# The batch loops of projection, attention and output of an adaLN transformer block, written out on every engine

## The chip, the core and the metric

The kernel runs on one core of one Trainium2 chip. The core has five engines, each with its own instruction sequencer and its own instruction stream: TensorE (PE, matrix products; its weight loads are listed as PEld), VectorE (DVE), ScalarE (ACT), GpSimd (POOL) and SyncE (SP, which here only issues DMAs). The streams meet at semaphores. The metric is the device time of one execution in microseconds; less is better.

## What is computed

The reference is a transformer block with adaptive layer norm: 16 batches of 1024 tokens, model width 256, 16 heads of 16, causal attention with rotary embedding, then a sparse feed-forward part over the first 2048 tokens.

```python
x = L0_attn_x                                   # (16, 1024, 256)
mod = (silu(c) @ wmod).reshape(16, 6, 1, -1)    # sa, ca, ga, sb, cb, gb
h = layernorm(x) * (1 + ca) + sa
# attention: q, k, v = layernorm(h) @ W + b; rope on q and k
scores = einsum('bhid,bhjd->bhij', q, k) / sqrt(16)      # causal mask
out = softmax(scores) @ v
x = x + ga * (h + out @ Wo + bo)
h = layernorm(x) * (1 + cb) + sb
x = x + gb * ffn(h)          # 8 experts, 512 gathered tokens each, gelu
```

## The kernel before

`build` runs five stages one after the other, each in a block of its own: `phase0` (weights and modulation), `phase1` (layer norms, projection, rotary embedding, splitting q and k into bf16 parts), `phase2` (attention), `phase3` (output projection and residual) and `phase4` (feed-forward). The text calls the middle three the projection, attention and output stages. The order of every engine's work is written by hand: each engine has a function that issues its own instructions and waits on semaphores whose target values are worked out from the batch number.

In these three stages the batches beyond the first few are driven by a hardware loop, `eng.Fori(lo, hi)`: the body stands once in the engine's program, a register holds the batch number, and at the end of the body the sequencer adds one and branches back. Every wait whose target depends on the batch needs that target computed in a register. Every engine has a loop of its own, and they are not tied to one another by anything but the work's semaphores.

- Projection: `run` (L343) writes out batches 0 to 2 and the last two, and loops over `it` from 1 to 6, two batches in a turn, on DVE, ACT, POOL and PE (L350). SP loops over `it` from 1 to 5 (L400). On DVE each batch is eight tiles of `rotate` (L474, L475, L481), `take_rest` (L490), the layer norm's statistics (`take_h`, L443) and `front_xn` (L461). POOL makes `h` (L625, L627) and the third part of q and k (L641).
- Attention: the work is 64 units, four head groups in each of 16 batches. A unit on PE has 40 score tiles (`scores_for_exp`, L1060), among them the filling of the maxima's banks for the unit two ahead (`fill`, L1035 and L1042), and 10 products of probabilities with v (`weigh`, L1079). ACT takes the exponentials of the 40 tiles (L997), DVE reduces the maxima (L951), POOL cuts the diagonal (L890). `steps` (L817) drives SP, POOL and DVE: batch 0 written out, a loop over batches 1 to 14, batch 15 written out. PE has the same shape (L1107 to L1113), and ACT writes out batch 0 and loops over 1 to 15 (L1009). A turn of these loops is one batch, four units.
- Output: `loop` (L1146) writes out batches 0 and 1 and loops over `it` from 1 to 7, two batches in a turn, on DVE, ACT and PE (L1149). SP loops from 1 to 6 (L1170). DVE's last step of each tile is L1203.

A loop of n turns takes its branch back n - 1 times and falls through at the last. For PE that is 5 times in the projection stage, 13 times in the attention stage and 6 times in the output stage. ACT's attention loop has 15 turns, so it branches back once more than PE's.

Of the kernel before, what the change touches and what calls it, by code (L numbers as in the profile page):

```python
# [27 lines left out]
NG = 4  # L28
# [245 lines left out]
def phase1(nc, x, ps, ident, rope, w_all, bias3, ones3, mods_d, resid_d, q_d, k_d, v_d):  # L274
    B, L, D = x.shape
# [7 lines left out]
    with ExitStack() as ctx:  # L283
# [59 lines left out]
        def run(eng, front, both, tail):  # L343

            front(batch(0, 0))
            both(batch(0, 1), batch(0, 0), first=True)
            both(batch(0, 2), batch(0, 1))
            with eng.Fori(1, B // 2 - 1) as it:  # L350
                both(batch(it, 1), batch(it, 0))
                both(batch(it, 2), batch(it, 1))
            last = B // 2 - 1
            both(batch(last, 1), batch(last, 0), more=False)
            both(None, batch(last, 1), more=False)
            tail(batch(last, 1))

        @block.sync
        def _(sp):
# [37 lines left out]
            load(batch(0, 2))  # L397
            step(0, 0)
            step(0, 1)
            with sp.Fori(1, B // 2 - 2) as it:  # L400
                step(it, 0)
                step(it, 1)
            step(B // 2 - 2, 0)
# [313 lines left out]
def phase2(nc, B, L, ps, ident, mask, q_d, k_d, v_d, max_d, att_d):  # L717
# [49 lines left out]
    AHEAD = 2  # L767

    with ExitStack() as ctx:
# [27 lines left out]
        LAST = B - 1  # L797
# [19 lines left out]
        def steps(eng, prologue, step, epilogue=lambda: None):  # L817

            prologue()
            for n in range(NG):  # L820
                step(unit(0, n), unit(0, n + AHEAD))
            with eng.Fori(1, LAST) as b:
                for n in range(NG):
                    step(unit(b, n), unit(b, n + AHEAD))
            for n in range(NG):
                step(unit(LAST, n), unit(LAST, n + AHEAD) if n + AHEAD < NG else None)
            epilogue()

        @block.sync
# [149 lines left out]
        def _(act):  # L979
# [24 lines left out]
                        copy_out(un, 0)  # L1004
                    exp(un, i)

            for n in range(NG):
                step(unit(0, n), None, first=(n == 0))
            with act.Fori(1, B) as b:  # L1009
                for n in range(NG):  # L1010
                    step(unit(b, n), None)
            copy_out(unit(LAST, NG - 1), 1)

        @block.tensor
        def _(pe):
# [88 lines left out]
                        weigh(prior(un), NPC + i - LAG)  # L1104

            prologue()
            for n in range(NG):  # L1107
                step(unit(0, n), unit(0, n + AHEAD), first=(n == 0))
            with pe.Fori(1, LAST) as b:
                for n in range(NG):  # L1110
                    step(unit(b, n), unit(b, n + AHEAD))
            for n in range(NG):
                step(unit(LAST, n), unit(LAST, n + AHEAD) if n + AHEAD < NG else None)  # L1113
            for i in range(NPC - LAG, NPC):
                weigh(unit(LAST, NG - 1), i)

# [2 lines left out]
def phase3(nc, B, L, D, ps, ident, wo, ones3, mods_d, out_bias_d, resid_d, att_d, sum_d, out):  # L1119
# [5 lines left out]
    with ExitStack() as ctx:  # L1125
# [20 lines left out]
        def loop(eng, work):  # L1146
            for p in range(2):
                work(p, 0, p)
            with eng.Fori(1, B // 2) as it:  # L1149
                for p in range(2):  # L1150
                    work(it * 2 + p, it, p)

# [6 lines left out]
        @block.sync  # L1159
        def _(sp):  # L1160
            def store(b, p, dst):
                sp.wait_ge(x2_done, b * T + T)
                sp.dma_start(dst.rearrange("(t p) d -> p t d", p=P), x2[:, p]).then_inc(stored[p], DMA)

            load(sp, 0, 0)
            load(sp, 1, 1)
            for p in range(2):
                store(p, p, sum_d[p * L:(p + 1) * L] if p < SB else out[p])
                load(sp, p + 2, p)
            with sp.Fori(1, B // 2 - 1) as it:  # L1170
                for p in range(2):
                    store(it * 2 + p, p, out[it * 2 + p])
                    load(sp, it * 2 + p + 2, p)
            for p in range(2):
                store(B - 2 + p, p, out[B - 2 + p])
            for p in range(2):
                sp.wait_ge(stored[p], DMA * (B // 2))
# [444 lines left out]
```

## Time and profile before

| | us |
|---|---|
| median of 3 runs | 3348.53 |
| range of the runs | 3348.07 to 3353.41 |
| the profiled execution | 3348.41 |
| its span, first to last instruction | 3346.70 |

So 1.7 us of the profiled execution lie outside its span, and it stands 0.1 us below the median. Durations and stretches below are from this execution. Projection takes about 79 to 745 us of the span, attention 825 to 2716 us, output 2733 to 3001 us. [...]

### The profile page before, as it was taken

The numbers are of one execution on the slowest core, as the hardware profiler recorded it, in microseconds if no ns is written. First come the engines' busy times: TensorE is split into PE (matmuls) and PEld (weight loads), VectorE is DVE, ScalarE is ACT, GpSimd is POOL, SyncE is SP. The second block draws the span as 40 slices with busy tenths as digits, with TensorE's granted clock in tenths as the row PEclk, the third lists the DMA queues.
The fourth block names the chain that finished last, engine by engine and source line by source line (L and its number), as shares of the span: only waits on it lengthen the run. The fifth ranks groups of instructions, "written<-read, shape, count | busy, mean of one in ns | idle before, by whom it ended". The sixth has DMA issues, their size and how long they took to land. (4 is left out here: it accounts for less than half of the span.)

```text
span 3346.7 us, 60748 instructions
## 1 busy us (share of the span) xinstructions
PE 2990.9 (89%) x18199; PEld 1411.5 (42%) x18199; DVE 2337.2 (70%) x3444; ACT 1711.9 (51%) x3591; POOL 1020.0 (30%) x1366
## 2 busy tenths in 40 slices
PE   2888888886999999999999999999999969984997
PEld 0444444442443333343343333334334337763564
DVE  5999999976777777777777777777777615544221
ACT  1444444431776766676676676667667731111211
POOL 3888888852221212111122111111112100002232
PEclk7999999996999999999999999999999989997999
DMA  2566666656344444344443444434444236654332
GB/s 75 152 181 181 181 182 183 183 177 129 80 94 90 97 94 85 82 97 98 92 96 81 89 98 97 83 82 96 98 94 93 51 138 259 257 207 130 90 88 64
DMA packets 175399, 403.50 MB, mean 121 GB/s; under 512 B 34556, under 2 KB 87202, under 8 KB 158518
## 3 DMA queue, kind: packets, MB, share of 16 engines
q1 hardware_dynamic: 168984, 391.37, 45.6%
q0 software_dynamic: 6144, 8.52, 1.5%
q8 instruction: 169, 2.77, 0.3%
q14 instruction: 102, 0.84, 0.1%
HBM read 240.65 MB, written 161.31 MB: 120 GB/s over the span
## 5 line engine op out<-in xcount | busy, mean ns | idle before, releaser
L951 DVE TENSOR_REDUCE mx<-ps 128x2 f32<-128x1024 f32 (+3 forms) x1216 | 1372.7, 1166 | 475.6 <-PE ps L1042 377.2
L997 ACT ACTIVATE prob<-ps 128x512 f32<-128x512 f32 (+1 forms) x2560 | 1248.9, 561 | 625.0 <-PE ps L1060 620.0
L1035 PE MATMUL ps<-k_rows,q_rows 96*128 96x512 bf16 (+3 forms) x3072 | 918.9, 335 | 59.0 <-DMA k_rows<-k_parts 33.3
L1060 PE MATMUL ps<-q_rows,k_rows 99*128 99x512 bf16 (+3 forms) x3072 | 919.5, 333 | 45.9 <-issue 29.0
L890 POOL TENSOR_SCALAR_AFFINE_SELECT prob<-prob 128x512 f32<-128x512 f32 x512 | 319.9, 637 | 1539.6 <-ACT prob L997 1539.6
L1079 PE MATMUL ps<-prob,v_rows 128*32 128x512 f32 (+3 forms) x6144 | 639.7, 505 | 0.0
L1060 PEld LDWEIGHTS ps<-q_rows,k_rows 99*128 99x128 bf16 x3072 | 276.3, 99 | 644.9 <-ACT prob L997 419.5
L688 PE MATMUL ps<-w_all,x_t 128*128 128x512 f32 (+1 forms) x1024 | 429.1, 544 | 0.0
L1035 PEld LDWEIGHTS ps<-k_rows,q_rows 96*128 96x128 bf16 x3072 | 291.6, 99 | 292.1 <-issue 68.5
L1042 PE MATMUL ps<-mask_b,unit_b 128*128 128x128 bf16 (+2 forms) x1408 | 353.6, 251 | 0.0
L1079 PEld LDWEIGHTS ps<-prob,v_rows 128*32 128x32 f32 x6144 | 136.7, 110 | 254.9 <-issue 180.8
L688 PEld LDWEIGHTS ps<-w_all,x_t 128*128 128x128 f32 x1024 | 183.6, 200 | 125.6 <-issue 104.1
L481 DVE TENSOR_TENSOR qr<-m 128x256 f32<-128x256 f32 x256 | 226.5, 967 | 4.4
L641 POOL TENSOR_TENSOR stage<-rest,stage 128x512 bf16<-128x512 f32 x128 | 168.0, 1313 | 121.9 <-ACT stage L575 121.8
L1214 ACT COPY n_t<-ps 128x256 f32<-128x256 f32 x128 | 47.7, 373 | 235.0 <-PE ps L1236 235.0
L1042 PEld LDWEIGHTS ps<-mask_b,unit_b 128*128 128x128 bf16 x1408 | 142.0, 101 | 24.1
L1482 DVE SCALAR_TENSOR_TENSOR y<-ps,gx,gate 128x256 f32<-128x256 f32 x32 | 15.5, 484 | 195.5 <-PE ps L1573 195.5
L1248 PE MATMUL ps<-wg,n_t 128*128 128x256 f32 x512 | 145.7, 407 | 0.0
L561 ACT COPY v_st<-ps 128x256 f32<-128x256 f32 x128 | 47.8, 374 | 178.1 <-PE ps L688 178.1
L675 PE MATMUL ps<-ident,xn 128*128 128x128 f32 x256 | 55.7, 303 | 87.5 <-DVE xn L461 87.5
L1203 DVE TENSOR_TENSOR x<-ps,res_b 128x256 f32<-128x256 f32 x128 | 54.3, 424 | 106.1 <-PE ps L1248 106.1
L1573 PE MATMUL ps<-w,hid 128*128 128x256 f32 x512 | 119.1, 386 | 0.0
(143 smaller groups left out, 2706.8 us busy)
## 6 DMA issues: line engine op xcount, KB each, us to landing
k_rows<-k_parts SPq DMA_DIRECT2D x384, 128.0 KB, 7.3
v_ones<-v_st SPq DMA_DIRECT2D x64, 512.0 KB, 8.5
v_rows<-v_ones SPq DMA_DIRECT2D x64, 512.0 KB, 8.9
att<-o_sb SPq DMA_DIRECT2D x128, 256.0 KB, 2.8
att_b<-att SPq DMA_DIRECT2D x16, 2048.0 KB, 9.6
q_parts<-stage SPq DMA_DIRECT2D x192, 128.0 KB, 2.3
k_parts<-stage SPq DMA_DIRECT2D x192, 128.0 KB, 2.4
q_rows<-q_parts SPq DMA_DIRECT2D x64, 384.0 KB, 4.6
```

The lines of the kernel that those rows point to most:

```text
L481: ins = dve.tensor_tensor(dst[:, :, :, :, e], src(m1)[:, :, :, :, e], src(m2)[:, :, :, :, 1 - e], ALU.add)
L641: pool.tensor_tensor(stage[:, p, 2, :, t * P:(t + 1) * P], rest[:, t % 2, :].rearrange("p (a n) -> p a n", a=4), stage[:, p, 1, :, t * P:( ...
L688: ins = pe.matmul(o, x_t[:, t % 2, k, :], w_all[:, k, lo:hi], start=False, stop=(k == KC - 1))
L890: pool.affine_select(out=own, in_=own, compare_op=ALU.is_ge, fill=0.0, base=0, pattern=[[0, HG], [1, P]], channel_multiplier=-1).then_inc( ...
L951: dve.tensor_reduce(dst, src, AX.X, ALU.max).then_inc(a_free, 1)
L997: nc.scalar.activation(prob[:, (g * NPC + i) % RING, h, 0:w], src, ACT.Exp).then_inc(exp_done, 1)
L1035: ins = pe.matmul(ps[:, at, col:col + w], q[0:ROWS, g, h, i * P:(i + 1) * P], k[0:ROWS, g, h, k0:k0 + w], start=(r == 0), stop=True, skip_ ...
L1042: ins = pe.matmul(own, unit_b[:, :], mask_b[:, :].rearrange("p (o n) -> p o n", o=1) .to_broadcast([P, per, P]), start=False, stop=True, s ...
L1060: ins = pe.matmul(ps[:, PS_B + bank(g, n), at:at + w], k[0:AUG, g, h, j * P:(j + 1) * P], q[0:AUG, g, h, q0:q0 + w], start=True, stop=True)
L1079: ins = pe.matmul(ps[32 * h:32 * h + 32, PS_O, col:col + w], v[:, g, j, h, :], prob[:, (g * NPC + i) % RING, h, at:at + w], start=(j == 0) ...
L1248: ins = pe.matmul(o, n_t[:, r % 2, k, :], wg[:, p, k, :], start=False, stop=(k == KC - 1))
L1573: ins = pe.matmul(o, hid[:, f, c * P:(c + 1) * P], w2[:, e % 2, f, :], start=False, stop=(f == FT - 1))
```

## The change

Every `Fori` of the three stages becomes a Python `for` with the same bounds, so each engine's program holds every batch's instructions in a row. In the attention stage the three pieces (first batch, loop, last batch) become one loop over the 64 units. Batch numbers are now plain numbers, so waits have constant targets, DMAs have constant addresses, and no register arithmetic and no backward branch is left. The order of the work on each engine stays as it was. The first and last stages are not touched.

```diff
@@ run, phase1: DVE, ACT, POOL, PE
-            with eng.Fori(1, B // 2 - 1) as it:
+            for it in range(1, B // 2 - 1):
                 both(batch(it, 1), batch(it, 0))
                 both(batch(it, 2), batch(it, 1))
@@ sync, phase1
-            with sp.Fori(1, B // 2 - 2) as it:
+            for it in range(1, B // 2 - 2):
                 step(it, 0)
                 step(it, 1)
@@ steps, phase2: SP, POOL, DVE (PE the same, with first=(u == 0))
-            for n in range(NG):
-                step(unit(0, n), unit(0, n + AHEAD))
-            with eng.Fori(1, LAST) as b:
-                for n in range(NG):
-                    step(unit(b, n), unit(b, n + AHEAD))
-            for n in range(NG):
-                step(unit(LAST, n), unit(LAST, n + AHEAD) if n + AHEAD < NG else None)
+            for u in range(B * NG):
+                step(unit(0, u), unit(0, u + AHEAD) if u + AHEAD < B * NG else None)
@@ scalar, phase2
-            for n in range(NG):
-                step(unit(0, n), None, first=(n == 0))
-            with act.Fori(1, B) as b:
-                for n in range(NG):
-                    step(unit(b, n), None)
+            for u in range(B * NG):
+                step(unit(0, u), None, first=(u == 0))
@@ loop, phase3: DVE, ACT, PE (SP's loop over its stores the same)
-            with eng.Fori(1, B // 2) as it:
+            for it in range(1, B // 2):
                 for p in range(2):
                     work(it * 2 + p, it, p)
```

PE's program before, at the end of the attention loop's body: the last score tiles of a batch's fourth unit, the last product with v, and the step back. ISA and REGISTER_ALU are register work. After the branch the program stands at the written-out last batch.

```order
L50 REGISTER_ALU
L1060 MATMUL ps<-q_rows,k_rows 128x256
L1035 MATMUL ps<-k_rows,q_rows 128x512
L1042 MATMUL ps<-mask_b,unit_b 128x128
L1075 REGISTER_ALU
L1079 MATMUL ps<-prob,v_rows 32x512 x4
L1109 REGISTER_ALU
L1109 COMPARE_AND_BRANCH
L1060 MATMUL ps<-q_rows,k_rows 128x512
```

What went are REGISTER_ALU (three here) and the branch. PE's program before at the start of that body, to which the branch leads (its first ISA row):

```order
L1109 UNCONDITIONAL_BRANCH
L1109 ISA
L50 ISA
L1060 MATMUL ps<-q_rows,k_rows 128x512
L1023 ISA
L50 ISA
L1035 MATMUL ps<-k_rows,q_rows 128x128 x4
L1042 MATMUL ps<-mask_b,unit_b 128x512
```

The four ISA rows and the jump ahead of them are gone as well. PE's program after, between the fourth unit of batch 1 and the first unit of batch 2 (line numbers past the changed places are 8 lower):

```order
L1052 MATMUL ps<-q_rows,k_rows 128x256
L1027 MATMUL ps<-k_rows,q_rows 128x512
L1034 MATMUL ps<-mask_b,unit_b 128x128
L1071 MATMUL ps<-prob,v_rows 32x512 x4
L1052 MATMUL ps<-q_rows,k_rows 128x512
L1027 MATMUL ps<-k_rows,q_rows 128x128 x4
L1034 MATMUL ps<-mask_b,unit_b 128x512
```

The matrix products stand in the same order; what went are the branch and every register instruction between them. PE's program has 8992 such rows where it had 2237.

ACT's program before, at the end of its attention loop (the exponentials of a unit's last score tiles):

```order
L992 REGISTER_ALU
L997 ACTIVATE prob<-ps 128x256
L992 REGISTER_ALU
L997 ACTIVATE prob<-ps 128x256
L1009 REGISTER_ALU
L1009 COMPARE_AND_BRANCH
```

All four register and branch rows are gone after, and the exponentials follow one another.

## Rows read from the trace of the kernel before

**Rows 1.** The page: TensorE clock granted, in 40 slices of the span (tenths).
```profile
PEclk7999999996999999999999999999999989997999
```
**Rows 2.** Busy by stretch (us; busy us of PE, PEld, DVE, ACT, POOL; granted clock; DMA share; GB/s).
```profile
163.54:671.04 507.50, 448.48 (x1537) 220.32 (x1536) 490.38 (x996) 218.47 (x505) 411.48 (x480) 0.93 0.63 184
```
**Rows 3.** Loop lines' sequencer instructions, ns min/median/max: attention, projection, output loop of PE.
```profile
L1109 PEldq COMPARE_BRANCH  x14: 83/3538/3994, 1048.5 to 2601.6; - x14
...
L350 PEldq COMPARE_BRANCH  x6: 76/208/234, 240.0 to 662.8; - x6
...
L1149 PEldq COMPARE_BRANCH  x7: 83/215/234, 2797.4 to 2998.9; - x7
```
**Rows 4.** Timeline of PE at a turn of the attention loop (start, us, work, idle before).
```profile
1049.10 1.06 PE L1079 MATMUL ps<-prob,v_rows 128*32 128x512 f32 x8
1052.33 0.39 PE L1060 MATMUL ps<-q_rows,k_rows 99*128 99x512 bf16 x1 [2.16 <-issue]
...
1055.40 0.59 PE L1035 MATMUL ps<-k_rows,q_rows 96*128 96x256 bf16 x2 [1.35 <-DVE mx L951]
```
**Rows 5.** Timeline of ACT: the first exponentials of units 8 and 56.
```profile
1052.84 1.84 ACT L997 ACTIVATE prob<-ps 128x512 f32<-128x512 f32 x3 [3.52 <-PE ps L1060]
...
2486.70 1.84 ACT L997 ACTIVATE prob<-ps 128x512 f32<-128x512 f32 x3 [3.62 <-PE ps L1060]
```
**Rows 6.** Busy by stretch: attention units 2, 6, 7, 8, 59, 60 (first exponential to next unit's).
```profile
881.09:909.29 28.20, 28.14 (x219) 11.60 (x217) 21.99 (x23) 20.54 (x43) 5.64 (x10) 1.00 0.46 96
994.14:1022.38 28.24, 28.18 (x218) 11.57 (x216) 22.05 (x23) 20.43 (x43) 5.64 (x10) 1.00 0.46 97
1022.38:1052.84 30.46, 28.24 (x218) 11.55 (x216) 22.22 (x23) 20.43 (x43) 5.64 (x10) 1.00 0.41 91
1052.84:1085.40 32.56, 31.07 (x218) 12.56 (x216) 22.05 (x22) 20.70 (x43) 5.64 (x10) 0.90 0.40 83
...
2575.47:2604.89 29.42, 29.36 (x227) 12.24 (x225) 22.39 (x24) 20.43 (x42) 5.64 (x10) 1.00 0.46 92
2604.89:2632.50 27.61, 27.17 (x209) 10.80 (x207) 21.88 (x22) 20.18 (x42) 5.64 (x10) 1.00 0.48 99
```
**Rows 7.** Busy by stretch: before and in a fall of the clock; around the last turn.
```profile
825.70:1054.40 228.70, 225.30 (x1705) 92.63 (x1703) 177.10 (x178) 164.73 (x338) 45.14 (x80) 1.00 0.41 85
1054.40:1061.20 6.80, 5.80 (x34) 2.75 (x34) 2.21 (x4) 2.07 (x4) 0.64 (x1) 0.50 0.01 4
2494.80:2686.00 191.20, 184.81 (x1391) 72.39 (x1388) 130.57 (x132) 138.76 (x288) 38.86 (x69) 1.00 0.36 76
```
**Rows 8.** Instruction queues (packets, MB, share): 825 to 937, 1050 to 1170, 225 to 660 us.
```profile
q8 instruction: 6, 0.10, 0.4%
...
q8 instruction: 10, 0.16, 0.6%
...
q14 instruction: 1, 0.01, 0.0%
```
**Rows 9.** Busy by stretch: projection, one batch each (batches 1, 4, 5, 13 on DVE).
```profile
121.15:163.54 42.39, 36.84 (x129) 18.00 (x128) 40.71 (x84) 18.30 (x43) 34.35 (x40) 0.96 0.63 183
248.33:290.84 42.51, 37.66 (x128) 18.67 (x128) 40.64 (x84) 18.41 (x44) 34.34 (x40) 0.92 0.63 182
290.84:332.92 42.08, 37.26 (x130) 18.29 (x128) 41.12 (x84) 18.02 (x42) 34.20 (x40) 0.92 0.63 184
629.07:671.04 41.97, 37.31 (x129) 18.27 (x128) 41.04 (x83) 18.11 (x42) 34.19 (x40) 0.92 0.63 193
```
**Rows 10.** Timeline of DVE: its wait for POOL in batches 4 and 5.
```profile
255.37 0.75 DVE L443 BATCH_NORM_STATS2 sth<-h 128x6 f32<-128x256 f32 x2 [1.29 <-POOL h L627]
...
297.56 0.75 DVE L443 BATCH_NORM_STATS2 sth<-h 128x6 f32<-128x256 f32 x2 [0.50 <-POOL h L627]
```
**Rows 11.** Busy by stretch: output, batches 2 and 3 (L1203 to L1203); a turn ends in 3.
```profile
2770.40:2787.05 16.65, 15.63 (x90) 11.80 (x89) 9.33 (x26) 2.98 (x8) 0.00 (x0) 1.00 0.69 259
2787.05:2804.00 16.95, 15.63 (x90) 11.81 (x89) 9.43 (x26) 2.98 (x8) 0.00 (x0) 1.00 0.70 259
```

More of the change, by code:

```diff
@@ L1106, in _ @@
             prologue()
[L1107 to L1113, printed above, removed]
+            for u in range(B * NG):
+                step(unit(0, u), unit(0, u + AHEAD) if u + AHEAD < B * NG else None, first=(u == 0))
             for i in range(NPC - LAG, NPC):
@@ L1169, in _ @@
                 load(sp, p + 2, p)
-            with sp.Fori(1, B // 2 - 1) as it:
+            for it in range(1, B // 2 - 1):
                 for p in range(2):
```

## Prediction

> **What bounds the kernel now.** I read the profile in four steps: which engine is full in each of the three stages, what the sequencers do at the loop lines, what the engines do around such a turn, and how long a unit of work is with and without one.
>
> Projection is bound by DVE: busy 490.38 of 507.50 us over batches 2 to 13 [rows 2]. Output is bound by PE: its products cover 15.63 of 16.65 us of a batch [rows 11]. Attention is bound by PE, and almost completely: in a unit of 28.24 us its products cover 28.18 [rows 6]. So in attention every microsecond that PE stands still is a microsecond of the span.
>
> The loop lines show where it does. PE's branch back takes 3.54 us in the median of the attention loop and 83 ns where it falls through, but 0.21 us in the projection and output loops [rows 3]. Around the first turn PE finishes the last product with v, then stands 2.16 us with "issue" as the reason: nothing that the profile knows of holds it, its program is missing. Less than 4 us later it stands again for 1.35 us, for DVE, which got its first bank late [rows 4]. [...]
>
> The instruction queues tell why only this loop pays. In one turn of the attention loop queue 8 moves 10 blocks; in the written-out batch 0 of the same stage 6; in 435 us of projection none, and the other instruction queue 1 [rows 8]. I read queue 8 as PE's own. A body that short enough is kept is run again at no cost, and the attention body of PE is not kept: it comes in anew each turn, and only the first block after the jump is waited for, since the others are fetched while PE works.
>
> [...]
>
> **The attention stage, step by step.** A turn's cost is read from starts of units on ACT. Units without a turn take 28.24 us, inside the loop; the unit before the first turn takes 30.46 and the one after it 32.56 [rows 6]. The excess is 2.22 us of standing and 4.32 us of slow clock, 6.54 together. Over many turns: unit 8 starts at 1052.84 and unit 56 at 2486.70 [rows 5], 48 units and 12 turns further, so a batch takes 1433.86 / 12 = 119.49 us against 4 x 28.24 = 112.96 without a turn. That is 6.53 us for each turn, the same number, so the first is no exception. 13 turns x 6.53 = 84.9 us.
>
> The last turn is different: PE falls through, and only ACT branches back. Units 59 and 60, between whose first exponentials it lies, take 29.42 + 27.61 = 57.03 us [rows 6] against 2 x 28.24 = 56.48, so ACT's own miss costs 0.55 us here. The clock stays at 1.00 through it [rows 7], so the fall belongs to PE's stop and not to ACT's. At the other 13 turns ACT's miss lies beside PE's and is in the 6.53 already. The branches of DVE, POOL and SP wait for no block.
>
> What is late next? If nothing stops PE, it goes on as between units 6 and 7. There PE waits for nobody, so I need no other engine to be faster. DVE has 22.0 of 28.2 us and ACT 20.5 [rows 6]. SP's loads of a unit's q, k and v are issued four units ahead and the maxima's round trip two units ahead; neither is moved relative to the products, and the stretch of eight units from 825.7 to the first turn shows no wait at full pace.
>
> The register work: PE loses thousands of small sequencer instructions, all waits become constants. Its price is seen by comparing a written-out unit with a looped one: unit 2 takes 28.20, unit 6 takes 28.24 [rows 6]. For the 56 looped units this is 0 to 0.04 x 56 = 2.2 us. It is hidden by PE's products, which fill the unit either way. I take 1.0.
>
> **Projection.** The turn itself costs DVE about 0.1 us (batch 5 takes 42.08 and ends in a turn, batch 13 takes 41.97 and ends in the fall-through [rows 9]), 5 x 0.1 = 0.5 us. The loop has two kinds of batch, 42.51 and 42.08 us, and the written-out batch 1 takes 42.39 [rows 9]. They differ in DVE's wait for POOL's `h`, 1.29 or 0.50 us [rows 10], which depends on how the two engines happen to stand to each other; I can't say which kind the new program falls into. If all 12 batches are of the written-out kind the stage takes 12 x 42.39 = 508.7 against 507.5, 1.2 us more; if all are of the short kind, 12 x 42.0 = 504, 3.5 us less. I take 0.5 less, close to the written-out rows, and keep both ends.
>
> **Output.** A batch takes 16.65 us without a turn and 16.95 with the first one [rows 11]. 6 turns x 0.30 = 1.8 us. The register work here I take at nothing, as it fits beside PE's products in attention.
>
> **What it adds.** Instructions that were kept now stream in: in projection and output no block came in during the loops, and now each batch brings its own. The nearest rows are written-out batches of the same stages, which ran from freshly fetched code: 42.39 us [rows 9], and 28.20 for attention [rows 6]. So this is hidden by work already queued, and I cost it at nothing. As a share of the DMA engines the instruction queue has 0.6% in its busiest stretch [rows 8].
>
> **Sum.** 84.9 + 0.55 + 1.0 + 0.5 + 1.8 = 88.75 us off. Profiled execution: 3348.4 - 88.75 = 3259.7. The median of the runs is 0.1 us above it; rounded, 3260.
>
> **Rivals.**
>
> *The clock falls anyway.* If the 6.8 us of half clock are a rhythm of the chip or of its power, they stay, and only the standing goes: 13 x 2.22 + 0.55 + 1.0 + 0.5 + 1.8 = 32.7, time 3316. For it: the clock falls in projection too [rows 1]. Against it: there PE also stands still each batch, the falls in attention follow each turn by the same few microseconds, and 228.7 us before the first turn and 191.2 us around the fall-through pass at 1.00 [rows 7]. A part of it is likelier than the whole: a run of 1700 us at full clock is seen nowhere in this trace, so the clock might fall a few times more. 4%.
>
> *The stream is too slow.* This one would make it slower. PE stops at the end of a block because the next is not there, as at the turn. A stop with its clock fall costs 6.5 us in attention, so the saving is gone at 88.75 / 6.5 = 14 stops. The attention stage brings in about 6 x 16 = 96 blocks; if one in four stopped PE, that is 24 x 6.5 = 156 us, time 3260 + 156 = 3416. Against it: 6 blocks came in during batch 0 and 9 of the 10 in each turn, and no unit there was longer than 28.24 [rows 6, 8]. It decides from the point at which a block arrives later than PE has run through the one before it; with 10 blocks in a batch of 119.49 us that is some 12 us. 2%.
>
> *A new wait appears in long steady running.* Today each turn gives the other engines 6.5 us to catch up. If one of them falls behind slowly, its wait shows after more than 8 units. With 1 us in each of 14 batches, time 3274; DVE and ACT have 6 us free in each unit, so I see no candidate but the DMAs. 8%.
>
> *It does not do what it says.* If the branch's cost stayed, in another form (the program split in parts with jumps between), the time would be 3346 or so. The program's order shows no jump inside the stages. 1%.
>
> *The projection turns cost as much as the attention turns.* If each of PE's 5 turns there held the stage up by what it does in attention, 5 x (3.54 - 0.21) = 16.7 us more would go, time 3243. Against it: the branches there take 0.21 us, DVE and not PE fills that stage [rows 2, 3], and batches with and without a turn differ by tenths [rows 9]. 1%. [...]
>
> **How the numbers follow.** The forecast, every turn's cost gone: 84%, own range 3255 to 3264, from 2.2 us of register work, -1.2 to 3.5 of projection, and a few us of spread between runs, whose highest before stood 4.9 above the median. To hold 8 in 10 with room for a wait in steady running I widen upward: 3253 to 3274. A measurement of this kernel can tell about 0.2%, 6.7 us, from no change. Slower by more takes the second rival, 2%; within it takes the last, 1%; all else is faster, 97%.
>
> **What would show it.** Right: PE has no idle of 2 us with "issue" in attention; the clock row reads 9 or more in every slice of that stage; all but the first and the last two or three of the 64 units take 28.2 us; the attention stage is 85 to 88 us shorter; projection and output change by less than 4 us each; queue 8 brings blocks in all three stages. Wrong: gaps on PE once in every block of its program (second rival), falls of the clock without a gap ahead of them (first), or a wait of PE for q, k, v or maxima from DMA (third).

## The result, and the profile of the changed kernel

The changed kernel takes 3257.19 us (median of 4 runs, 3256.85 to 3258.85), the kernel before, run beside it, 3349.84 us (4 runs, 3348.07 to 3353.41). The ratio is 0.9723, 95% interval 0.9706 to 0.9740. The forecast was 3260. The profiled executions take 3256.85 and 3348.41 us, with spans of 3255.1 and 3346.7.

The first look goes to the clock and the instruction queues. Lines of the page of the changed kernel, as [rows 1] for the clock:

```profile
span 3255.1 us, 50330 instructions
...
PEclk7999999996999999999999999999999989987999
...
q8 instruction: 147, 2.41, 0.3%
q14 instruction: 98, 0.80, 0.1%
```

The clock row looks almost like the one of before: a slice is 81 us long, and a fall of 6.8 us in it leaves a 9. The queues brought 147 and 98 blocks (before: 169 and 102), so fewer than with the loops: writing out projection and output brings 20 blocks more on queue 8 (189 in the fourth run below), but the attention body no longer comes in 14 times. That queue 8 is PE's shows in the runs below: from 830 to 2650 us it brings 147 blocks in the kernel before, 109 with PE's attention loop alone written out (run one) and 148 with ACT's alone (run two).

The stretches show it better. Busy by stretch of the changed kernel: units 2, 7 and 8 of attention (the last at a place where the loop turned before), then 1771.5 us on end, then a batch of projection and one of output, to be set against [rows 6, 7, 9, 11]:

```profile
852.32:880.52 28.20, 28.14 (x219) 11.61 (x217) 21.99 (x23) 20.53 (x43) 5.62 (x10) 1.00 0.46 96
...
1021.52:1049.72 28.20, 28.14 (x219) 11.60 (x217) 21.99 (x23) 20.53 (x43) 5.63 (x10) 1.00 0.44 96
1049.72:1077.92 28.20, 28.14 (x219) 11.61 (x217) 22.00 (x23) 20.53 (x43) 5.63 (x10) 1.00 0.48 96
826.20:2597.70 1771.50, 1761.93 (x13439) 723.97 (x13437) 1364.24 (x1367) 1291.02 (x2643) 354.38 (x630) 1.00 0.45 92
121.50:163.70 42.20, 37.28 (x129) 18.21 (x128) 40.56 (x84) 18.11 (x42) 34.34 (x40) 0.92 0.63 184
2681.61:2698.18 16.57, 15.63 (x90) 11.83 (x89) 9.33 (x27) 2.98 (x8) 0.00 (x0) 1.00 0.70 262
```

The units around a batch's start were 30.46 and 32.56 us long [rows 6]; they are 28.20 now, like units 4 to 61 without exception. The granted clock is 1.00 for 1771.5 us, where before it fell 13 times. The timeline of PE at the start of batch 2 has no idle time in brackets, where [rows 4] has two:

```profile
1048.29 1.07 PE L1071 MATMUL ps<-prob,v_rows 128*32 128x512 f32 x8
1049.29 0.39 PE L1052 MATMUL ps<-q_rows,k_rows 99*128 99x512 bf16 x1
1049.52 0.39 PE L1027 MATMUL ps<-k_rows,q_rows 96*128 96x128 bf16 x4
```

Where the 91.6 us of span went, between the same instructions of both kernels: attention from unit 4 to unit 63 88.04, projection (batch 0 to batch 15 on DVE) 0.72, output (batch 0 to batch 15) 2.32, and the seams and the end together 0.5. So the total is near the forecast, and nearly all of it in attention. The experiments ask whether it went for the reasons given: which engine's loop pays, what the second stop of PE is, and what the slow clock costs.

To read a turn, I take from each trace its cost: from the start of unit 4b-1 to that of unit 4b+2 on ACT (b is the batch that begins there), less three units without a turn (28.24 us, or 28.20 where ACT's loop is written out). In the kernel before the 13 costs lie between 6.21 and 6.77, 6.51 on average, and each has a fall of the clock of 6.8 us. These costs come from one profiled execution of each kernel.

### The profile page after: what moved, and what is told of

It reads as the page before. It is cut to its first block and busy times, and to the rows that moved or that the text cites. A ratio compares the mean times of both kernels' runs of the same rounds, so it can differ in the third digit from the quotient of the medians.

```text
span 3255.1 us, 50330 instructions
## 1 busy us (share of the span) xinstructions
PE 2952.9 (91%) x18199; PEld 1403.3 (43%) x18199; DVE 2328.9 (72%) x3444; ACT 1713.4 (53%) x3591; POOL 1019.2 (31%) x1366
## 5 line engine op out<-in xcount | busy, mean ns | idle before, releaser
L1052 PE MATMUL ps<-q_rows,k_rows 99*128 99x512 bf16 (+3 forms) x3072 | 908.5, 329 | 14.5 <-ACT prob L992 6.0
L1071 PE MATMUL ps<-prob,v_rows 128*32 128x512 f32 (+3 forms) x6144 | 628.6, 497 | 0.0
L641 POOL TENSOR_TENSOR stage<-rest,stage 128x512 bf16<-128x512 f32 x128 | 167.5, 1308 | 119.3 <-ACT stage L575 119.2
```

Of the source, the lines that this page charges most:

```text
L641: pool.tensor_tensor(stage[:, p, 2, :, t * P:(t + 1) * P], rest[:, t % 2, :].rearrange("p (a n) -> p a n", a=4), stage[:, p, 1, :, t * P:( ...
L1052: ins = pe.matmul(ps[:, PS_B + bank(g, n), at:at + w], k[0:AUG, g, h, j * P:(j + 1) * P], q[0:AUG, g, h, q0:q0 + w], start=True, stop=True)
L1071: ins = pe.matmul(ps[32 * h:32 * h + 32, PS_O, col:col + w], v[:, g, j, h, :], prob[:, (g * NPC + i) % RING, h, at:at + w], start=(j == 0) ...
```

## Experiments: which loop pays

**One. PE's attention loop alone written out.** Projection, output and the other engines' attention loops stay.

```
...
-            with pe.Fori(1, LAST) as b:
-                for n in range(NG):
-                    step(unit(b, n), unit(b, n + AHEAD))
...
+            for u in range(B * NG):
+                step(unit(0, u), ...)
```

> Only PE's attention loop is written out; every other loop stays. Theory (the cost is PE's stop at its own branch back, plus the slow clock behind it): 13 turns x 6.53 us go and 2.2 us of register work, but ACT still branches back 14 times and its miss, now uncovered, costs 0.55 us each time (it costs that in the kernel before where PE falls through): 3348.4 - 84.9 - 2.2 + 13 x 0.55 = 3268. No fall of the clock in attention. Rival (the cost belongs to a turn as such, taken by all engines together, whoever branches): little changes, 3330 to 3348.

Measured: 3271.1 us (3269.79 to 3273.6), ratio 0.9768 (0.9751 to 0.9784). Busy by stretch, unit 6 and the two units around ACT's first turn:

```profile
994.28:1022.52 28.24, 28.18 (x218) 11.57 (x216) 22.06 (x23) 20.43 (x43) 5.63 (x10) 1.00 0.47 97
1051.79:1081.06 29.27, 28.98 (x221) 11.94 (x220) 22.91 (x23) 21.77 (x45) 5.62 (x10) 1.00 0.47 93
1081.06:1108.67 27.61, 27.55 (x212) 11.11 (x211) 21.43 (x23) 19.86 (x42) 5.63 (x10) 1.00 0.50 98
```

No fall of the clock is left in attention. Two things stay. ACT's turn, uncovered now, costs 29.27 + 27.61 - 56.48 = 0.40 us the first time and 0.43 on average over the 13. And a unit is still 28.24 us long, although PE has no register work any more.

**Two. ACT's attention loop alone written out.** The same edit on ACT.

> Only ACT's attention loop is written out. Theory: ACT's miss lies beside PE's in 13 of 14 turns and only the last one's 0.55 us goes: 3347 to 3348. Rival (ACT's miss of 2.6 us is part of what holds PE up, or makes the clock fall): up to 13 x (3.52 - 1.30) = 29 us less, 3319.

Measured: 3340.01 us (3338.7 to 3342.42), ratio 0.9971 (0.9960 to 0.9982). Its unit 6, by stretch:

```profile
994.12:1022.32 28.20, 28.14 (x219) 11.60 (x217) 22.06 (x23) 20.53 (x42) 5.63 (x10) 1.00 0.46 97
```

My expectation of 3347 to 3348 was missed, for two reasons. The 0.04 us a unit are ACT's register work and not PE's: they go here, and did not in the first run. That is 56 x 0.04 = 2.2 us. Nearly all the rest of the 9.7 us of span is in the turns: 77.9 us for 13 instead of 84.6, since three of the falls last 3.4 us and not 6.8. The prices of the three such turns average 4.94 us, those of the ten others 6.31. That was the first sign that the clock's part is no fixed price.

**Three. Attention written out on all engines.**

> All five engines' attention loops written out, projection and output loops kept. Theory: attention holds 88 of the 91.6 us by which the spans differ: 3257.2 + 0.7 + 2.3 = 3260. Rival (writing out projection and output matters by more than their own stretches show, through what the next stage finds): off by more than 3 us from that.

Measured: 3263.25 us (3262.47 to 3265.13), ratio 0.9741 (0.9725 to 0.9757). What is left for projection and output is 3263.25 - 3257.19 = 6 us, and I had expected 3; by the mark that I had set, 3 us, that is a miss. Attention from unit 4 to unit 63 takes 1663.84 us here, the same as in the changed kernel, and projection and output 2.4 us more. Of the 8.3 us by which the two spans differ, 4.3 lie in the passage from projection to attention: from the first rotation of batch 15 to the first exponential it takes 118.4 us here, 114.1 in the changed kernel and 113.7 to 116.4 in the other runs. Why it varies is not shown.

**Four. Projection and output written out, attention left as it was.** The edit is the other half of the diff.

> Projection and output loops written out on all engines, attention loops kept. Theory: the stretches of projection and output differ by 0.7 and 2.3 us between the two traces, so 3348.4 - 3.0 = 3345.4. The two parts add up: this saving and that of the kernel with only attention written out sum to the whole, 91.6 us, within 2 us. Rival (the new streaming of instructions costs something that attention's gain hid): 3349 or more.

Measured: 3307.33 us (3306.5 to 3310.89), ratio 0.9877 (0.9860 to 0.9893). My expectation fell: 43 us instead of 3. Of the 41.8 us of span nearly all, 41.5, is in attention (unit 4 to unit 63), whose code is untouched and whose branches take as long as before. Nor do the two parts add up: runs three and four save 87 and 43 us, the whole change 93. The sequencer's branch at the attention loop line:

```profile
L1109 PEldq COMPARE_BRANCH  x14: 83/3580/3885, 1050.6 to 2561.7; - x14
```

And PE around the first turn:

```profile
1051.19 1.06 PE L1079 MATMUL ps<-prob,v_rows 128*32 128x512 f32 x8
1054.72 0.39 PE L1060 MATMUL ps<-q_rows,k_rows 99*128 99x512 bf16 x1 [2.46 <-issue]
...
1056.09 0.38 PE L1060 MATMUL ps<-q_rows,k_rows 99*128 99x512 bf16 x1
1056.31 0.38 PE L1035 MATMUL ps<-k_rows,q_rows 96*128 96x256 bf16 x2
```

The first stop is there, the second of [rows 4] is not: the product of L1035 follows at once. The clock falls at 5 of the 13 turns only. The 8 turns without a fall cost 2.48 us on average, four with a fall of 3.4 us 3.90, one with a fall of 6.8 us 5.47.

**Five. Two batches a turn in attention, on PE and ACT.** 7 turns instead of 14, 6 jumps back of PE instead of 13.

> PE's and ACT's attention loops take two batches in a turn (7 turns), all else as before. PE then branches back 6 times. Theory (a price of 6.53 us for each branch back of PE, and its body starts at the same place of its program as before): 7 x 6.53 = 45.7 us go: 3304. Rival (the price hangs on how many instructions come in, and as many come in as before): no change, 3350.

Measured: 3302.65 us (3301.67 to 3303.18), ratio 0.9864 (0.9847 to 0.9882). The six turns that remain inside the loop cost 6.22 us each with a fall of 6.8 us, the seven places between them nothing. The price belongs to the jump, not to the number of units.

## Experiments: what the second stop is

What differs between the fourth kernel and the one before is where in PE's program the attention body lies. A new theory follows. The second stop, which the profile lays to DVE, is the end of the first block that was brought after the jump. For it speaks the kernel before itself. Its DVE at the first turn, and its instruction queues in the 8 us around it (each digit and each GB/s is 0.2 us):

```profile
1048.43 2.36 DVE L951 TENSOR_REDUCE mx<-ps 128x2 f32<-128x1024 f32 x2 [0.92 <-PE ps L1042]
1053.86 1.23 DVE L951 TENSOR_REDUCE mx<-ps 128x8 f32<-128x1024 f32 x1 [3.07 <-PE ps L1042]
```

```profile
DMA  0000000301000000000001030000000000000000
GB/s 0 0 0 0 0 0 0 82 0 41 0 0 0 0 0 0 0 0 0 0 0 41 0 82 0 0 0 0 0 0 0 0 0 0 0 0 0 0 0 0
...
q8 instruction: 2, 0.03, 1.9%
q14 instruction: 2, 0.02, 0.7%
```

The profile lays the stop to the second of these reductions, which ends at 1055.09. But by the kernel's code the product of 1055.40 needs only the last reduction of the unit before, the first row here, and that had ended by 1050.79, 4.6 us earlier. Queue 8 brought two blocks: the first from 1049.50 to 1050.63, the second from 1052.74 to 1054.01. PE went on at 1052.33 and at 1055.40, 1.7 and 1.4 us after each had landed (over the 13 turns 1.6 to 1.8, and 1.2 to 1.6). The second stop also ends later where its block lands later. Counted from PE's first restart, the block landed after 1.45 to 1.49 us in five turns and PE went on after 2.80, once 3.07; it landed after 1.81 to 1.92 in four and PE went on after 3.07 to 3.35. DVE's reduction ended after 2.76 in all 13. And at each of the 13 turns the second stop comes behind the same instruction, the 32nd after the branch in the trace.

**Six and seven. Empty instructions ahead of the loop.** 48 and 256 of them were written at the head of PE's attention program, to shift the body. That 256 are one block, as the second expectation has it, is what the changed kernel's trace gives: from 880 to 2500 us queue 8 brings 99 blocks, and PE executes 12,367 products, 12,364 weight loads and some 630 semaphore operations, 256 traced instructions a block.

> The kernel before with 48 empty instructions ahead of PE's attention work, where PE waits for DMA anyway; they move the loop's body 48 instructions on in PE's program. New theory: PE stops twice at a turn, both times for its program. The second stop, 32 instructions into the body, is the end of the first block that came in; moved on by 48, the body starts just behind such an end, has a nearly whole block ahead, and the second stop goes. The clock then mostly stays up. As in the kernel with projection and output written out, whose body was moved too, 3.2 us a turn are left: 3350 - 13 x 3.2 = 3309. Rival (the second stop is a wait for DVE, as the profile has it, or the other kernel's gain came from something else than the place of the body): 3350.

> As the kernel with 48 empty instructions, but 256 of them: one whole block. Theory: the body stands at the same place of a block as in the kernel before, so both stops and the fall of the clock are back at all 13 turns: 3350, 32 instructions from branch to second stop. Rival (empty instructions as such change the time, by a shift of the stage or of the engines to one another): as with 48 of them, or another time.

Measured: 3350.52 us (ratio 1.0007, 0.9997 to 1.0016) and 3349.58 us (1.0002, 0.9991 to 1.0012). These two say nothing on the theory. The empty instructions never reached the executed program: PE's sequencer shows 925 semaphore and 3775 register operations in all three traces. They are repetitions of the kernel before, and as such useful for two things. The falls lasted 88.8 us together in the profile of run seven and 78.5 us in that of run six, in which the first three turns had a fall of 3.4 us and the ten after them one of 6.8 us. And in two of those three (the turns into batches 2 and 4) there is no second stop. PE and DVE at the first of them:

```profile
1056.84 0.64 PE L1035 MATMUL ps<-k_rows,q_rows 96*128 96x256 bf16 x2
...
1056.66 1.23 DVE L951 TENSOR_REDUCE mx<-ps 128x8 f32<-128x1024 f32 x1 [4.11 <-PE ps L1042]
```

The clock fell there as PE went on after the first stop, at 1054.08, so PE ran slowly and came to this product only 1.4 us after the second block had landed (1055.42). It did not stop, and it started before DVE's reduction was done. So PE was not waiting for that reduction, in a program that is the same as before.

**Eight. Empty instructions at the 13 places of the changed kernel.**

> The changed kernel with 60 empty instructions on PE at each of the 13 places where it branched back before. [...] Theory (a standstill of PE is what counts, whatever makes it): PE idles 1.3 to 4.3 us at each place; if it is over 3 us, the clock falls each time, and the loss is idle plus 4.3 us, 13 x 7 = 91, time 3348; if it is about 2 us, the clock falls at some places only and the loss is 13 x 2.5 to 13 x 5: 3290 to 3320. Rival (the fall of the clock needs the fetching, not the standstill): no fall in the stage at any length, loss 13 x idle alone.

Measured: 3257.72 us, ratio 0.9731 (0.9713 to 0.9748), the changed kernel again, for the same reason (1411 semaphore operations in both). So no run shows the 1.3 to 4.3 us of idle with which the expectation reckons; what stops of 1.93 and 3.51 us cost is shown by run ten.

**Nine. 24 real products ahead of the loop.** Nothing reads what they write.

```
                 pe.wait_ge(consts, 2)
+                for _ in range(24):
+                    pe.matmul(ps[:, PS_O, 0:P], unit_b[:, :], unit_b[:, :], start=True, stop=True)
```

> The kernel before with 24 matmuls more (unit_b by unit_b into the bank of the outputs, nobody reads them) at the head of TensorE's attention program, where it waits for the first k_rows anyway. They are executed, 24 weight loads and 24 matmuls, and only move the loop's body by 48 instructions. The loop stays. Theory: the second stop of each turn, which in the kernel before always stands 32 instructions behind the branch, is the end of the first piece of program that was brought, and not a wait for VectorE; with the body moved by 48 that end comes some 240 instructions behind the branch and the second stop is gone. The first stop of 2.0 to 2.6 us stays, the clock falls at a part of the 13 turns only, and the attention stage gets 30 to 45 us shorter, as in the run with only projection and output written out: 3310 (3300 to 3325). Rival: the second stop belongs to the order of the work (the buffer that VectorE frees) or the gain of that run came from the stages before, then nothing changes: 3349, with 13 falls of 6.8 us.

Measured: 3312.57 us (3309.57 to 3314.07), ratio 0.9885 (0.9869 to 0.9902). First that they ran, then the branch, then PE at the first turn:

```profile
L1087 PE MATMUL ps<-unit_b x24: 287/314/314, 768.9 to 771.4; 128*128 128x128 bf16 x24
```

```profile
L1111 PEldq COMPARE_BRANCH  x14: 83/3588/4050, 1050.9 to 2564.8; - x14
```

```profile
1054.90 0.39 PE L1060 MATMUL ps<-q_rows,k_rows 99*128 99x512 bf16 x1 [2.36 <-issue]
...
1056.24 0.38 PE L1060 MATMUL ps<-q_rows,k_rows 99*128 99x512 bf16 x1
1056.46 0.38 PE L1035 MATMUL ps<-k_rows,q_rows 96*128 96x256 bf16 x2
```

Adding 48 instructions makes the kernel 37 us faster, with the loop in place: the same work in the same order, the branch as dear as ever, and no second stop at any of the 13 turns. The rival, that the order of the work or DVE makes it, is out. Here too the price depends on the clock: 6 turns without a fall cost 2.31 us each, five with 3.4 us of fall 4.03, two with 6.8 us 5.69.

## Experiments: what the clock does when PE stands still

**Ten. Waits put into the changed kernel.** PE waits for a memset by POOL at the 13 places; no block of program is waited for.

```
+        KINDS = ((2300,), (2300, 3500), (4200,))
+        HALTS = {b * NG: KINDS[(b - 2) % 3] for b in range(2, B - 1)}
...
+                    for at, n in enumerate(HALTS[un[2]]):
+                        pool.memset(spare[:, at, 0:n], 0.0).then_inc(halt, 1)
...
+                        if (i, h) == (0, 0) and un[2] in HALTS:
+                            pe.wait_ge(halt, halts(un[2]) + 1)
+                        if (i, h) == (0, 3) and len(HALTS.get(un[2], ())) > 1:
+                            pe.wait_ge(halt, halts(un[2]) + 2)
```

> The changed kernel, nothing looped, with waits put in at the 13 places where TensorE branched back before (starts of batches 2 to 14): TensorE waits for a GpSimd memset of a scratch tile that nobody reads. Three kinds in turn. Batches 2, 5, 8, 11, 14: one memset of 2300 elements a partition, by the profile's memsets (4096 elements 3.54 us, 8192 6.93 us, 256 0.32 us) about 2.0 us, so one stop of about 2.1 us. Batches 3, 6, 9, 12: the same and a second of 3500 elements (3.0 us) that releases TensorE 32 instructions later: two stops of about 2.1 and 1.4 us, as in the kernel before. Batches 4, 7, 10, 13: one of 4200 elements, a stop of about 3.6 us. No program is fetched at these places. Theory: the granted clock falls because TensorE stands still, whatever the reason, and twice in a row or long is worse than once short: the places with two stops show 6.8 us at 0.50 and cost about 6.5 us each as the turns before did, the short ones fall at two in five at most and cost 2.1 to 2.6, the long ones fall for 3.4 us mostly and cost 5 to 7: 3257 + 4 x 6.5 + 5 x 2.4 + 4 x 6 = 3319 (3305 to 3335). Rival: a wait at the same place lets the clock alone and only the fetch brings it down: the stops alone, 5 x 2.1 + 4 x 3.5 + 4 x 3.6 = 39 us: 3296, no fall at the 13 places.

Measured: 3310.96 us (3307.96 to 3311.81), ratio 0.9881 (0.9865 to 0.9898). In the profile the 13 places cost 52.5 us. Of the five stops of 1.93 us four brought the clock down for 3.4 us (3.6 us each) and one did not (1.99). Of the four stops of 3.51 us three brought it down for 6.8 us (6.1 us each) and one did not (3.58). Of the four pairs, laid out as 1.93 and 0.91 us, three brought 3.4 us and one none. The total came out as expected (3319, 3305 to 3335), but not its parts: I had taken the pairs for the dearest, and the long single stops are. Two of these, for batches 4 and 7, in PE's timeline, and then a stretch of 6.8 us in or around each:

```profile
1287.76 0.61 PE L1061 MATMUL ps<-q_rows,k_rows 99*128 99x512 bf16 x1 [3.51 <-POOL spare_h L906]
```

```profile
1639.50 0.39 PE L1061 MATMUL ps<-q_rows,k_rows 99*128 99x512 bf16 x1 [3.51 <-POOL spare_h L906]
```

```profile
1286.20:1293.00 6.80, 5.24 (x24) 2.75 (x28) 1.56 (x2) 2.39 (x4) 1.74 (x2) 0.50 0.00 0
1636.00:1642.80 6.80, 3.30 (x32) 1.98 (x36) 2.38 (x3) 2.34 (x4) 3.72 (x2) 1.00 0.01 2
```

The same stop, the same work around it, and once the clock goes to 0.50, from 1286.20 on and so before the stop ends, and once it stays at 1.00. So the fall needs no wait for program; PE's standing still for 1.93 us is enough to bring it, at four of five places. But it does not bring it every time.

**Eleven. Six batches a turn in projection and output.** How long may a body be before its branch costs something?

> The kernel before, with the projection's and the output's loops turning once for six batches instead of once for two (2 turns each), attention untouched. It tells how long a body may be before a branch back costs something. The projection's body on TensorE is then about 1740 instructions instead of 580, the output's about 1220 instead of 407; the attention's of 2002 costs 3.3 to 4.0 us a branch in the kernel before and the projection's of 580 0.21 us. Theory A (what counts is the length): the 1740 is on the far side too, a branch of some 3 us once in the projection, with a clock fall. Theory B (the limit lies higher, between 1740 and 2002): 0.2 us as before. Either way the stage changes by less than 7 us: the projection's stretch 548 to 555 us. Attention's own body is moved by it as well, so its 13 turns may again show one stop instead of two, 3310 then and 3345 otherwise.

Measured: 3336.36 us in one run. The branch at PE's projection loop line, at its output loop line, and DVE's at the same output line:

```profile
L350 PEldq COMPARE_BRANCH  x2: 83/1915/3747, 410.2 to 672.7; - x2
```

```profile
L1153 PEldq COMPARE_BRANCH  x2: 76/150/223, 2876.8 to 2985.5; - x2
...
L1153 DVEq COMPARE_BRANCH  x2: 55/64/74, 2878.9 to 2987.6; - x2
```

The 1740 instructions of the projection body are too many (3.75 us, against 0.21 before), the 1220 of the output body are not (0.22 us): the limit of PE lies between. Yet output is 7.6 us longer than in the kernel before and projection 8.5, each with one turn where it had six and five, and it is not PE that pays first. In output DVE, whose body is now 270 instructions where it was 90, stands 2.8 us after its branch and stops a second time soon after, with nothing to wait for (queue 14 brings 4 blocks from 2870 to 2900 us; in the kernel before it brought none from 2800 to 3000 us):

```profile
2882.08 0.76 DVE L1191 TENSOR_TENSOR wg<-wo,gate_b 128x256 f32<-128x256 f32 x2 [2.79 <-issue]
...
2886.55 0.26 DVE L1199 RECIPROCAL rec<-ps 128x16 f32<-128x16 f32 x1 [3.71 <-issue]
...
2887.41 0.29 PEld L1242 LDWEIGHTS ps<-ident,norm 128*128 128x128 f32 x2 [7.95 <-DVE norm L1203]
```

In projection, where its body has 750 instructions and its branch lies at 416.6, DVE does the same, and these two stops are nearly all of the 8.5 us:

```profile
421.59 0.20 DVE L436 RECIPROCAL rsx<-sd 128x8 f32<-128x8 f32 x1 [3.43 <-issue]
...
426.76 0.69 DVE L476 TENSOR_TENSOR m<-ps,rope 128x512 f32<-128x512 f32 x1 [4.77 <-issue]
```

DVE's body of 250 in the projection loop of before is kept, 270 is not; so its limit is lower than PE's. DVE's branch itself takes 0.06 to 0.07 us all the same: its miss shows only in the idle time behind. My bound of 7 us a stage was too low because I looked at PE alone. Attention gets 32 us shorter again, with one stop a turn: a third place of the body, and a third time without the second stop.

**Twelve. Two waits in the sizes of before at all 13 places.** The tenth kernel with one kind, 2576 and 4030 elements.

> The changed kernel with two waits put in at all 13 places where TensorE branched back before, in the sizes of the two stops of the kernel before: memsets of 2576 and 4030 elements a partition for stops of 2.16 and 1.35 us (2300 and 3500 gave 1.93 and 0.91 us in the run before). No program is fetched there. Theory: the price of a turn in the kernel before (6.5 us) comes whole from TensorE standing still for 3.5 us in two pieces; the granted clock falls for 6.8 us at nearly every place and the time goes back by 13 x 6.5 = 84.5: 3342 (3325 to 3348). Rival: two stops cost here what they cost at the four places of the run before (3.1 to 3.6 us each with 2.84 us of standing still, the clock down for 3.4 us or not at all), plus 0.7 us for their greater length: 13 x 4.2 = 55: 3312 (3305 to 3318), and what brought the clock down for 6.8 us at every turn of the kernel before is more than the standing still.

Measured: 3318.23 us (3316.28 to 3319.77), ratio 0.9910 (0.9893 to 0.9927), beside 3348.67 for the kernel before. The stops came out as meant at eight places. PE at batch 3:

```profile
1169.47 0.39 PE L1061 MATMUL ps<-q_rows,k_rows 99*128 99x512 bf16 x1 [2.16 <-POOL spare_h L906]
...
1172.87 0.39 PE L1061 MATMUL ps<-q_rows,k_rows 99*128 99x512 bf16 x1 [1.35 <-POOL spare_h L906]
```

By stretch, the unit before and the unit after the first stop, of batch 3 and of batch 6:

```profile
1139.48:1169.90 30.42, 28.20 (x219) 11.64 (x217) 22.25 (x23) 20.54 (x42) 8.32 (x12) 1.00 0.43 89
1169.90:1199.62 29.72, 28.31 (x219) 11.52 (x217) 21.82 (x22) 20.59 (x42) 8.55 (x11) 1.00 0.45 91
1489.12:1519.54 30.42, 28.20 (x219) 11.65 (x217) 22.26 (x23) 20.53 (x42) 8.31 (x12) 1.00 0.44 89
1519.54:1551.44 31.90, 31.08 (x219) 12.37 (x217) 21.82 (x22) 20.80 (x42) 8.56 (x11) 0.89 0.41 84
```

Eight places without a fall cost 3.75 us each, four with 6.8 us of fall 5.96, one with 3.4 us 3.83: 57.7 us together. The theory asked for 84.5 and does not hold as it stood; the rival's 55 is nearer, but it expected no falls of 6.8 us. Both had a fixed price for the clock, and there is none: the first stop and the two waits are the same 13 times over, and the clock falls at 5 of them. It falls before the second stop: at four places 1.2 to 1.5 us after the first has ended, at batch 2 just before its end. PE then comes late to the second wait, which leaves a stop of 0.64 to 1.00 us, and none at batch 2. Batch 6:

```profile
1522.51 0.61 PE L1061 MATMUL ps<-q_rows,k_rows 99*128 99x512 bf16 x1 [0.76 <-POOL spare_h L906]
```

Where the clock does fall for 6.8 us, the place costs nearly what a turn of before cost, 5.96 against 6.51. So the price of a turn can be taken apart: some 3.75 us for standing still twice, the rest for the clock.

## Why the prediction was right, and where not

**The turns (13 x 6.53 = 84.9).** Right: the costs of the 13 turns add up to 84.6 us in the kernel before and all of it is gone, since PE has neither a jump nor a stop left. Runs one and five confirm that the price belongs to PE's jump.

**Its two parts (2.22 of standing, 4.32 of slow clock).** This split was wrong, though the sum was not touched by it. I took the excess of the unit after the turn for the clock's whole, but the second stop lies in that unit. With two stops and no fall a place costs 3.75 us (run twelve); the clock's share of 6.51 is thus some 2.8 us. The first rival's 3316 hung on the split: with 3.75 for 2.22 it would have been 3296. Nor had PE stood still twice when the clock fell: in the kernel before each fall begins 1.45 to 2.16 us after the end of the first stop, at most 0.45 us into the second.

**The second stop ("for DVE, which got its first bank late").** Wrong. It is PE's own program again, the end of the first block. Run nine takes it away with 48 instructions ahead, at an unchanged order of work. Had I looked up in the code which reduction the product needs, and set its end, 1050.79, against 1055.40, I would have seen it before. With it falls "only the first block after the jump is waited for": the second is waited for too. The reading matters for other changes: a faster DVE would have gained nothing here, and a shift of the body gained 37 us.

**ACT's last turn (0.55).** Read rightly; 0.43 on average where it stands alone, in run one.

**Register work (0 to 2.2, taken as 1.0).** 2.2, the upper end, and it is ACT's and not PE's (runs one and two). "It is hidden by PE's products, which fill the unit either way" was the failed step: it can't be hidden if units are shorter without it. The 28.20 of the written-out unit was the row to go by, 56 times.

**Projection (0.5, between -1.2 and 3.5).** 0.72 between the two profiles. Over all runs it is less: from batch 0 to batch 15 the five profiles with this stage written out take 630.55 to 631.14 us, the eight with its loop as it was 630.89 to 631.53, 0.3 more on average. The two kinds of batch are gone, though neither won: batches 1 to 13 all take 42.22 to 42.27 us, between 42.08 and 42.51. The wait of [rows 10] is now 1.29 or 1.30 us where I looked, in batches 4 and 7.

**Output (1.8).** 2.32. I left out its register work: a batch without a turn takes 16.57 us and not 16.65.

**What it adds, at nothing.** Right. All three stages run from newly fetched program without a stop; 1771.5 us at clock 1.00 exclude the second rival.

**The sum.** 88.75 us were forecast and 91.6 of span measured. Most of the 2.8 between them is register work (1.2 more), output (0.5) and projection (0.2). Another 0.5 is unit 62, which took 28.72 us before and takes 28.24 now, and 0.5 the seams between the stages; neither was in the sum, and why unit 62 was longer is not shown.

**The rivals.** *The clock falls anyway* was wrong as a rhythm of the chip, since not one fall is left in 1771.5 us. But I had argued against it with a fixed link, that the falls "follow each turn by the same few microseconds", and that link is loose: in runs four and nine most turns had a fall of 3.4 us or none. *A new wait in long steady running* did not come: units 4 to 61 all take 28.20 us. *The projection turns cost as much* is refuted by the 0.72 us. Nor does a jump as such cost PE what it costs in attention: a body of 580 traced instructions jumps back in 0.21 us and one of 1220 in 0.22, one of 1740 in 3.75 and one of 2002 in 3.5.

**What stays open.** Why the clock fell at every one of 13 turns before, and with two waits of the same length put in by hand at 5 of 13. In the kernel before the turns follow each other at an even 119.5 us and each fall begins 5.4 to 6.0 us after the branch; in run twelve the places are 116.6 us apart, and 118.7 after a fall. In run six, the kernel before once more, the first four turns are 116.8 to 118.0 us apart and the first three falls last 3.4 us; from there on it is 119.2 to 120.0 and 6.8. When a stop comes may matter beside how long it is. That is a guess: the profile does not show what the chip looks at, and no run changed the spacing alone. Nor was the body shifted by one whole block, which should bring the second stop back. The limits of a body's length come from one body on each side, and whether its place in the program moves them no run shows.

## What to carry to other kernels

Look at the time of a loop's branch on the sequencer that bounds the stage, and write the loop out, or make its body short enough, where the branch takes microseconds: here 3.5 us of branch were 6.5 us of time. Look also for idle time laid to "issue" behind the branch, since DVE's branches took 0.07 us where DVE then stood for 2.8 and 3.7. PE and DVE had different limits here (between 1220 and 1740 traced instructions, and between 250 and 270), and the longer body pushed DVE past its own. When the profile lays an idle time to a semaphore, look up in the code which value is waited for, and check when it was reached; here it was reached 4.6 us earlier, the stop came behind the 32nd instruction at each of 13 turns, and it was the program that was late. An unrelated edit that shifts the code can change such a loop's kernel by 1% (43 us in run four, 37 in run nine), so compare variants by stage and by turn and not by totals alone.

## What the runs showed of the hardware

- PE goes on 1.2 to 1.8 us after the block that it waits for has landed, in both stops of all 13 turns of the kernel before.
- PE keeps a body of 1220 traced instructions and not one of 1740 (branches of 0.22 and 3.75 us, run eleven); DVE keeps 250 (kernel before) and not 270 (stops of 2.8 and 3.7 us, run eleven). A miss shows in the time of PE's branch (3.3 us and more) but not in that of DVE's (0.07 us).
- The second block lands 5.2 to 6.1 us after the branch (kernel before, 13 turns). PE stops for it when it comes early to the end of the first block: at all 13 turns there, at 11 of 13 in run six, where the slow clock made PE late at the other two.
- Standing still for 1.9 to 3.5 us, for program or for POOL, brings PE's granted clock from 1.00 to 0.50 for 3.4 or 6.8 us, or not at all (13 falls at 13 turns before, 5 at 13 in run four, 10 at 13 places in run ten, 5 at 13 in run twelve). A product of 128x512 stands in the trace with 0.61 us at 0.50 and 0.39 at 1.00. With a single stop of some 2.3 us a turn costs 2.3 to 2.5 us without a fall, 3.9 to 4.0 with one of 3.4 us and 5.5 to 5.7 with one of 6.8 us.
- At full pace PE held 1.00 for 1771.5 us.
